# DLRM tower on one core: the quarters of the first layer moved from between the turnings to behind the first four gram parts, and the second layer from behind the first part to behind the sixth

## The reference, cut to what matters

```
e = stack([tbl_f[ids[:, f]] for f in 0..31], axis=1)       # [2048, 32, 256]
dots = einsum('bnd,bmd->bnm', e, e)                         # [2048, 32, 32]
z = dots[:, iu, ju]                                         # 496 pairs, i < j
h = concatenate([z, dense_ctx], axis=1)                     # [2048, 512]
h = maximum(h @ W_top1 + b_top1, 0)                         # [2048, 512]
h = maximum(h @ W_top2 + b_top2, 0)                         # [2048, 256]
y = h @ W_top3                                              # [2048, 1]
```

## Time and profile before

| what | value |
|---|---|
| median of the three runs | 896.8 us |
| the profiled execution | 895.49 us |
| its span on the core | 893.7 us |
| PE busy, matmuls | 588.3 us (66%), 11019 |
| POOL busy, gathers | 399.7 us (45%), 419 gathers of 0.95 us |
| ACT busy | 205.5 us (23%) |
| DVE busy | 224.9 us (25%) |
| mean granted TensorE clock | 0.845 |

### The profile page before, as it was taken

How to read it: one execution, slowest core, us unless ns; L and a number is a source line. 1 busy time by engine, 2 the same in 40 slices (tenths; PEclk the granted TensorE clock), 3 DMA queues, 4 the chain that set the end, 5 groups by cost and what they waited for, 6 DMA issues and landing times.

```text
span 893.7 us, 24184 instructions
## 1 busy us (share of the span) xinstructions
PE 588.3 (66%) x11019; PEld 519.5 (58%) x11019; DVE 224.9 (25%) x578; ACT 205.5 (23%) x369; POOL 399.7 (45%) x426
## 2 busy tenths in 40 slices
PE   3557668385683847748487583876838568384797
PEld 2456557275572746737376473765727557274696
DVE  3344223123131231213222231222312313122122
ACT  4252303103040031301213022030310304003142
POOL 7563625526254362533626346262552625436210
PEclk9788969698796987969789697896969879698769
DMA  9962313313122231321313223131231312213110
GB/s 225 239 206 62 94 50 78 91 44 98 49 79 80 56 103 37 86 69 55 107 44 87 57 66 102 44 92 50 79 91 44 98 49 76 76 53 92 35 32 2
DMA packets 37459, 70.97 MB, mean 79 GB/s; under 512 B 10382, under 2 KB 23438, under 8 KB 37358
## 3 DMA queue, kind: packets, MB, share of 16 engines
q0 software_dynamic: 20112, 54.95, 21.9%
q1 hardware_dynamic: 17246, 14.48, 7.0%
HBM read 69.39 MB, written 0.01 MB: 78 GB/s over the span
## 4 chain that ended last, share of the span: by engine, by line
PE 54%; another core or an unknown queue 27%; issue 10%; ACT 6%; DVE 2%; ACTq 0%; DVEq 0%
PE look_ps L339 17%; PE quad_ps L359 15%; PE top_ps L421 6%; PE top_ps L408 5%; PE quad_ps L323 5%; PE turn_ps L323 4%; ACT turned L484 3%; PE top_ps L398 1%; ACT ahead L491 1%; ACT area L513 1%; PE quad_ps L378 1%; DVE small L665 1%; DVE one_hot L675 1%; ACT products L507 0%
## 5 line engine op out<-in xcount | busy, mean ns | idle before, releaser
L296 POOL DMA_INDIRECT rows<-in_tbl,row_ids x419 | 398.9, 952 | 457.4 <-PE turn_ps L323 160.2
L359 PE MATMUL quad_ps<-turned 128*32 128x31 f32 x7680 | 139.5, 205 | 216.4 <-ACT turned L484 149.8
L339 PE MATMUL look_ps<-one_hot,small 125*128 125x256 f32 (+1 forms) x1536 | 243.0, 304 | 51.4 <-issue 39.1
L359 PEld LDWEIGHTS quad_ps<-turned 128*32 128x32 f32 x7680 | 107.0, 116 | 254.3 <-ACT turned L484 154.7
L339 PEld LDWEIGHTS look_ps<-one_hot,small 125*128 125x128 f32 x1536 | 211.1, 203 | 64.1 <-issue 60.2
L675 DVE TENSOR_SCALAR one_hot<-ids_across,sub_row 125x256 fp32r<-125x256 int32 (+1 forms) x384 | 110.9, 362 | 149.6 <-PE look_ps L339 129.8
L491 ACT ACTIVATE ahead<-look_ps 128x512 f32<-128x512 f32 (+1 forms) x48 | 28.3, 590 | 269.2 <-PE look_ps L339 253.3
L484 ACT ACTIVATE turned<-turn_ps 128x512 f32<-128x512 f32 x57 | 34.7, 625 | 209.0 <-remote 104.6
L323 PE MATMUL turn_ps<-ident,rows 128*128 128x128 f32 x424 | 65.8, 284 | 23.3 <-DMA rows<-in_tbl,row_ids 13.3
L484 ACT ACTIVATE turned<-quad_ps 128x512 f32<-128x512 f32 x55 | 33.6, 627 | 185.6 <-remote 104.2
L408 PE MATMUL top_ps<-area,w_sb 128*128 128x128 f32 x488 | 65.1, 275 | 2.0 <-issue 1.2
(11 more groups left out here) (50 smaller groups left out, 153.8 us busy)
## 6 DMA issues: line engine op xcount, KB each, us to landing
rows<-in_tbl,row_ids POOLq DMA_INDIRECT x419
ids_across<-in_small_ids SPq DMA_DIRECT2D x45, 128.0 KB
landed<-in_tbl SPq DMA_DIRECT2D x6, 896.0 KB
w_sb<-in_W_top SPq DMA_DIRECT2D x4, 256.0 KB
landed<-in_tbl SPq DMA_DIRECT2D x6, 104.0 KB
w_sb<-in_W_top SPq DMA_DIRECT2D x1, 512.0 KB
area<-in_dense_ctx SPq DMA_DIRECT2D x16, 8.0 KB
row_ids<-in_ids SPq DMA_DIRECT2D x1, 240.0 KB
```

The lines of the kernel that those rows point to most:

```text
L296: pool.indirect_dma_start(out=rows[:, n % PLACES, j, :], out_offset=None, in_=tables[f], in_offset=bass.IndirectOffsetOnAxis(ap=row_ids[:, ...
L339: last = pe.matmul(look_ps[:, c * width:(c + 1) * width], small[:, f, r, part, c * P:(c + 1) * P], one_hot[n % 2][:, r, 0:width], start=(r ...
L359: last = pe.matmul(gram_ps[q * FIELDS:(q + 1) * FIELDS, g // BANK_GROUPS, at:at + COLS], turned[:, c, s, :], turned[:, c, s, 0:COLS], star ...
```

## The change

The edits touch the orders of PE, ACT and DVE. Tiles 1 to 14 are concerned; in the last tile the order stays as it was.

- PE: the four quarters of layer 1 leave the turnings and stand behind gram parts 0, 1, 2 and 3. Layer 2 stands behind part 5 and no more behind part 0.
- ACT: `keep_hidden1(t - 1)` stands behind the copy of the tile's first look-up and no more ahead of it.
- DVE: `last_layers(t - 1)` stands behind the second one-hot matrix of the tile and no more behind the first.

```diff
+    LAYER2_BEHIND = 5
...
-                    if LAYER1_AFTER <= i < LAYER1_AFTER + M1:
+                    if t == TILES - 1 and LAYER1_AFTER <= i < LAYER1_AFTER + M1:
                         layer1(t - 1, i - LAYER1_AFTER)
...
                         gram(t, k)
                     else:
                         last_gram(k)
-                    if t > 0 and k == 0:
+                    if 0 < t < TILES - 1 and k < M1:
+                        layer1(t - 1, k)
+                    if t > 0 and k == (0 if t == TILES - 1 else LAYER2_BEHIND):
                         layer2(t - 1)
...
-                    keep_hidden1(t - 1)
+                    if t == TILES - 1:
+                        keep_hidden1(t - 1)
                 for n in range(FIRST[t], FIRST[t + 1] - 1):
                     keep_looked_up(n)
+                    if t > 0 and n == FIRST[t]:
+                        keep_hidden1(t - 1)
...
-                    if k == 0 and t > 0:
+                    if k == 1 and t > 0:
                         last_layers(t - 1)
```

## The result

The changed kernel takes 942.78 us (median of four runs, 942.34 to 944.24). The kernel before, timed beside it, took 896.73 us (median of four; one of the four, at 2103.77 us, lies far from the other three and is left out of the ratio). The ratio is 1.0532, with a 95% interval of 1.0515 to 1.0549: slower. The forecast was 924 us, in a range of 865 to 950. Its sign held, and of its mechanism the longer run and the later release; 28 us had been worked out, 46 were measured.

A forecast was written before the change was run, and what follows sets the result against it. Runs of gathers hold PE's signals back. Look-up 2.0, part 1 onward 23.3, quarters 2.7, layer 2 2.0, clock 1.5 give 31.5 us, +2.0 per tile; 14 tiles add 28 to 895.49: 924 us, range 865 to 950.

The forecast's parts named there:

- The cause: A run of back-to-back gathers holds PE's signals back, whatever PE computes; the quarters of layer 1 are not the cause.
- The start-up: A look-up PE records from 18.80 for 6.27 us is seen at 37.51, 12.4 us late, amid a run.
- Turnings: Three quarters leave from ahead of unit 12, which is then seen at about 430.7, not 446.3.
- POOL: The run grows to 18 gathers; PE is free of it at 448.8, 2.5 us later than before.
- What PE gets done inside the run: At 0.19 us of work per us, 3.4 us come through by 448.8; the second look-up piece starts then.
- The clock: If full clock returns at the same place, 3.1 us behind the look-up run at 1.2 GHz, losing 1.5 us.
- From part 1 on: PE needs 23.3 us to the next run, plus 2.7 for three uncovered quarters and 2.0 for layer 2.
- The upper bound: If only the look-up's first piece is done inside the run, part 0 and a quarter remain: +5.1 us per tile.
- The first: PE keeps its pace inside the run: about -8.5 us per tile, 776 us; chance of faster by over 2%: 0.25.
- The rule of the Trainium skill: Matmul signals follow within tens of ns (56 ns for one tile), so unit 12 would be seen at 427.9.
- The second rival: PE avoids 1.2 GHz or recovers at once: 0.0 us per tile, 895 us; chance within 2%, with lower bound: 0.27.
- the third: Unit 12 is still seen only when the run ends: +2.4 us per tile, 929 us; counted within the forecast's 0.48.

The follow-up runs named there:

- The kernel without gathers: Kernel before, and the changed kernel, with all gathers from the tenth unit on left out: 531.56 and 555.52 us.
- the run of sixteen: Changed kernel with the seventeenth gather made to wait for gram part 0: 897.54 us against 894.65, ratio 1.003.
- the run of fourteen: Kernel before with the fifteenth gather held back until PE has finished gram part 0: 850.7 us against 900.4, ratio 0.9474.
- the kernel with two units in flight: Kernel before, each unit's gathers waiting until the unit but one ahead has landed: 625.04 us against 561.12, ratio 1.1153.

## Why the prediction was right, and where it was mis-sized

**The cause.** That the run of gathers holds PE back, and not the quarters between the turnings, was read from the last tile and the start-up. The kernel without gathers, the run of sixteen and the run of fourteen bear it out. The release 3.9 us behind the run's last gather, read off once, is 3.91, 4.16, 3.86 and 3.78 us for runs of 16, 18, 16 and 14 in the tiles shown. It is steady: in the 14 tiles of before ACT's late copy starts 3.77 to 3.91 us behind the last gather, in those of the run of fourteen 3.71 to 3.82.

The start-up was read wrongly in one point. The late look-up is seen at 37.51, which is not in the midst of a run: the run's last gather had started at 31.79, and POOL then stood still as well.

```profile
31.79 0.95 POOL L296 DMA_INDIRECT rows<-in_tbl,row_ids  x1 [0.30 <-issue]
37.80 0.95 POOL L296 DMA_INDIRECT rows<-in_tbl,row_ids  x1 [5.06 <-remote]
```

That release comes 5.7 us behind the last gather, so the 3.9 us are no constant. The bytes may be the better mark. In the four tiles shown they stop arriving 1.4 to 1.8 us ahead of the release (at 444.75, 466.75, 446.5 and 423.5), while in the start-up, with SP's large loads beside the gathers, they still flow at 31.79 to 37.51. The end of the tile's run in before, by windows:

```profile
442.00:444.00 2.00, 0.00 (x0) 0.00 (x0) 0.00 (x0) 0.00 (x0) 1.04 (x2) 0.50 0.57 136
444.00:446.00 2.00, 0.00 (x0) 0.00 (x0) 0.00 (x0) 0.00 (x0) 0.00 (x0) 0.50 0.25 70
446.00:448.00 2.00, 0.89 (x42) 0.74 (x43) 0.00 (x0) 1.63 (x5) 1.16 (x2) 0.50 0.00 0
```

No run tests whether the release follows the landing of the last gather.

**Turnings.** Unit 12 was put at 7.1 us from the run's start (430.7 less 423.61) and is seen at 8.6. The count of matmuls was a fair guide, though not exact.

**POOL.** Eighteen gathers without a break were forecast, and are there. The release was put at 25.2 us from the run's start and is at 25.47.

**What PE gets done inside the run: this step failed in its size.** I took 0.19 us of work in 1 us, and so had the look-up, part 0 and a quarter done by the release. The rows after fit another measure better: PE gets through one to two *matmuls* in 1 us, short or long. Seventeen gram matmuls took 15 us, and by the free pace of part 1 (64 in 0.77 us, 473.47 to 474.24) they are 0.2 us of work. In the run of fourteen, ten of the look-up's matmuls start between 413.56 and 420.50, at 1.4 in 1 us, and each of those is eleven times as long. In before it was 1.7 in 1 us (twelve from 430.73 to 437.81) and then 1.4 (twelve to 446.30); they happened to be long ones, and I read a pace in work off them. With 25 matmuls of part 0 and the quarter left, 2.3 us stood in the open that I had counted as done.

**The clock.** I had it return 3.1 us behind the look-up, for a loss of 1.5 us. It returned at 473.7, just behind part 1's start. So nearly all of that term was not there, and the look-up ahead took 2.6 us and not 2.0. The 2.0 us were misread: I took them for the price at half clock, but in before that look-up (452.96 to 454.98) ran its second half behind 453.9, at full speed. Wholly at 1.2 GHz it takes 2.6 us, here and with layer 2 alone moved (450.18 to 452.83). Against before the stretch at 1.2 GHz has grown from 17.1 to 20.5 us.

**From part 1 on.** 23.3 + 2.7 + 2.0 = 28.0 us were worked out; 27.7 us are measured (473.47 to 501.20). Layer 2 takes 1.99 us, as said.

| term | forecast | measured |
|---|---|---|
| start of the run to release | 25.2 | 25.47 |
| rest of part 0 and a quarter | 0 | 2.26 |
| look-up | 2.0 | 2.62 |
| from part 1 to the next run, with the clock's term | 29.5 | 27.73 |
| tile | 56.7 | 58.08 |

The 1.4 us between them, 14 times, are 20 us: the 924 forecast against the 943 measured. That they are no more is partly luck: the release, part 0 and the look-up were 3.2 us too low, and the last term 1.8 us too high. The upper bound (+5.1 us) had been this very case, with nothing of part 0 done; with 39 of 64 done it is +3.4.

**The rivals.** The first, in which PE keeps its pace on short matmuls, is refuted by the 17 matmuls in 15 us, on the chips that withhold. On the others PE does keep its pace, with the old order (the kernel with two units in flight) and with the new one, and the change is slower there too, by 1.4 to 2.8%: that I had no case for. The wait for ACT behind it is a price that I had set at nothing, with the run as its cover, and I had not said what it costs if the run's hold is gone. The rule of the Trainium skill ("TensorE: Matmul & The Clock Gate", section "The cost: per-tile semaphore tail") goes with this rival. The last tile agrees with it, and so does the changed kernel where nothing is withheld: a turning that ends at 310.42 is copied by DVE at 310.46, beside gathers. The 15.7 us of the execution shown do not. The second rival, the clock that stays up, is refuted by 20.5 us at 0.50. Of the third, unit 12 seen only at the run's end, nothing came.

**What carries the loss.** I had booked the loss mostly to quarters without cover. The run of sixteen, with the same quarters in the same places, has none of it. The loss is the two gathers that join the run when unit 12 is seen early (2.8 us), and 0.7 us behind the release, most of it the look-up, which now runs at 1.2 GHz from end to end: the clock comes back 5.1 us after PE is let go, and in the run of sixteen after 3.5 us (at 451.5).

## What to carry to other kernels

A wait that one removes may have been the only thing that broke up another engine's run. Before removing it, ask what that engine will now do without a break and who is held meanwhile; a wait put in at the right place, as the fifteenth gather's here, was worth 5%. And time a kernel that leans on such an effect more than once and on more than one chip: here the kernel before took 895 to 900 us in the measurement of the result and on two chips of the experiments, and 561 to 562 us on two others.

## What the hardware showed that was not expected

- Indirect gathers, issued back to back by GpSimd, withhold the signals of TensorE's matmuls for up to 15.7 us, until 3.7 to 4.2 us after the last one has started (5.7 us in the start-up). While it lasts, PE's matmuls start at steps of about 0.71 us or twice that (452.35, 453.07, 453.78, 455.19) after a first batch of 22. Transfers of the same bytes that are not indirect do not (539 against 900 us). Why is open. So is whether the matmuls themselves are held up or only the news of them: in before PE records 30 matmuls behind unit 11 (from 429.06 to 435.67) before DVE sees that unit at 437.81, so a recorded start may run far ahead of what is finished. And a span and a clock are on record for every timed execution, so that the recording has a part in it is not excluded.
- It is not there on every chip: of the four in the experiments two withheld and two did not, with gathers at the same pace of one each 1.25 us. Each chip was used at one time only, so the moment could be what differs and not the chip. No run says what sets them apart.
- The release does not hang on what PE computes: it comes 3.8 to 4.2 us behind the last gather's start, whether PE's last recorded matmuls are look-ups (before, and the run of fourteen) or gram matmuls (after, and the run of sixteen).
